# Forward transform of the Fourier tower: the third quarter of a pair's pixels is turned ahead of the first result of the pair in front

## The chip, the cores and the metric

The kernel runs on one core of a Trainium2 chip, as one launch. The metric is the device time of that launch in microseconds; lower is better. Three runs of the kernel before give a median of 4477.31 us (4468.72 to 4491.48).

## What is computed

A four-layer Fourier tower over 64 images of 64 x 64 pixels, followed by attention and expert layers on its result. All numbers are float32. The part that matters here is this, cut from the reference:

```python
for l in range(LAYERS):                       # LAYERS = 4
    sc = _spectral_conv(h, w1r[l] + 1j * w1i[l], w2r[l] + 1j * w2i[l])
    pw = jnp.einsum('bihw,oi->bohw', h, pw_w[l]) + pw_b[l][None, :, None, None]
    y = sc + pw
    y = (y - mean(y)) * rsqrt(var(y) + EPS) * gamma[l] + beta[l]
    h = jax.nn.gelu(y, approximate=False)
```

`_spectral_conv` takes the two-dimensional Fourier transform of h, keeps 32 x 16 of its modes, multiplies each mode by a 64 x 64 complex matrix and transforms back.

## The kernel before

The 64 images are 32 **pairs** (`NP`); one pair is 128 partitions x 4096 pixels (two images of 64 channels), 2 MB. Four pairs (`Q`) are a group. Each layer has three stages, with a barrier of all engines between them (`phase_end`): **forward** (Fourier transform of h), **mix** (the products per mode) and **inverse**. For layer 0 the forward transform is done in another way; so the loop over layers (`Fori(1, L)`) runs the forward stage three times. This case is about that stage alone: `sync_forward`, `tensor_forward`, `scalar_forward` and `vector_forward`, lines 717 to 822.

What is done for a pair p in the forward stage, in the order of the data:

1. SP loads the pair from `y_dram` into one of four buffers, `hf[p % 4]` (L721). The load of pair p waits until all four quarters of pair p - 4 have been turned out of that buffer.
2. ACT applies scale, shift and Gelu in place, in four quarters of 1024 columns (L790).
3. VectorE **turns** each quarter: `px_turn(p, v)`, v = 0 to 3, a transpose in blocks of 32 x 32 from `hf` to `hT[p % 2]` (L795).
4. PE does the transform along the width, `w_dft(p)`: 32 products in the program, 64 matmul records in the trace (L750). It starts when all four quarters are turned and both results of pair p - 1 have been taken from its banks 0 to 3.
5. VectorE takes the result in two halves: `w_turn(p, 0)` from banks 0 and 1, then `w_turn(p, 1)` from banks 2 and 3 (L800).
6. PE does the transform along the height, `h_dft(p)`, 128 matmul records, into banks 4 to 7 (L767). It starts when both halves of step 5 are taken.
7. VectorE takes that with two transposes, `h_turn(p)` (L809), and once in four pairs SP stores the group's spectrum to `spec_in` (L726).

Each engine runs its instructions in the order in which they are written. PE goes `w_dft(p)`, `h_dft(p - 1)`, `w_dft(p + 1)`, and so on. VectorE's order is the loop at the end of `vector_forward`. Its step p of 34 handles three pairs at once: the pixels of pair p, the width result of pair p - 1 and the height result of pair p - 2:

```python
for p in range(NP + 2):
    # px_turn(p, 0), px_turn(p, 1),
    # w_turn(p - 1, 0), px_turn(p, 2),
    # w_turn(p - 1, 1), h_turn(p - 2), px_turn(p, 3)
```

In the text below a **cycle** is the stretch from the end of one `px_turn(p, 3)` to the end of the next; there are 31 in each forward stage, 93 in all.

Of the kernel before, what the change touches and what calls it, by code (L numbers as in the profile page):

```python
# [102 lines left out]
def build(nc, d, B, out):  # L103

    NP, NG = B // 2, B // GI
# [3 lines left out]
    with ExitStack() as ctx:  # L109
# [682 lines left out]
        def vector_forward(dve, lf):  # L792
            def px_turn(p, v):
                dve.wait_ge(f_ready, lf * (NP * 4) + (p * 4 + v + 1))
                dve.transpose(hT[p % 2][:, :, 16 * v:16 * v + 16, :].rearrange("p s h c -> p h s c"),  # L795
                              hf[p % Q][:, v * 2 * BK:(v + 1) * 2 * BK].rearrange("p (h s x) -> p h s x", h=16, s=2)).then_inc(px_turned, 1)

            def w_turn(p, i):
                dve.wait_ge(wdft_done, lf * (NP * 4) + (p * 4 + 2 * i + 2))
                dve.transpose(t1[p % 2][:, 2 * i:2 * i + 2].rearrange("p g a c h -> p (g a) c h"),  # L800
                              banks[:, 2 * i:2 * i + 2, :].rearrange("p b (a h c) -> p (b a) c h", a=2, c=CQ)).then_inc(wdft_turned, 1)

            def h_turn(p):
                g, q = p // Q, p % Q
                dve.wait_ge(hdft_done, lf * NP + (p + 1))
                if q == 0:
                    dve.wait_ge(spec_stored[g % 2], lf * (NG // 2 * 16) + (g // 2 * 16 + 16))
                for b in range(2):
                    dve.transpose(xs[g % 2][:, :, b * Q + q, :, :],  # L809
                                  banks[:, 4:8, b * 128:(b + 1) * 128].rearrange("p q (c k) -> p k q c", c=CQ)).then_inc(hdft_turned, 1)  # L810

            for p in range(NP + 2):
                for v in range(2):
                    if p < NP:
                        px_turn(p, v)
                for i in range(2):
                    if 0 < p <= NP:
                        w_turn(p - 1, i)
                    if i == 1 and p > 1:
                        h_turn(p - 2)  # L820
                    if p < NP:
                        px_turn(p, 2 + i)

# [1121 lines left out]
        @block.vector  # L1947
        def _(dve):
            vector_spectrum0(dve)
            phase_end(dve, 1)  # L1950
            vector_mix(dve, 0, True)
            phase_end(dve, 2)
            vector_inverse(dve, 0, True)
            dve.sem_inc(px_turned, 4 * Q)
            dve.sem_inc(wdft_turned, 2)
            dve.sem_inc(hdft_turned, 2)
            phase_end(dve, 3)
            with dve.Fori(1, L) as l:
                vector_forward(dve, l - 1)
                phase_end(dve, l * 3 + 1)  # L1960
                vector_mix(dve, l, False)
                phase_end(dve, l * 3 + 2)
                vector_inverse(dve, l, False)
                phase_end(dve, l * 3 + 3)
            vector_head(dve)
            phase_end(dve, TOWER + 1)
            tail_vector(dve)
# [71 lines left out]
```

## Time and profile before

| | |
|---|---|
| median of three runs | 4477.31 us (4468.72 to 4491.48) |
| the profiled execution | 4476.43 us, its span 4474.6 us |
| mean granted TensorE clock | 0.884 of full speed |
| busy: PE, PE weight loads, DVE, ACT | 76%, 49%, 53%, 47% of the span |
| forward stages (by their VectorE instructions) | 663 to 983, 1574 to 1894, 2486 to 2810 us |
| DVE in them, three stages | L795 447.0 us, L800 235.6 us, L809 123.4 us |
| DMA | 1119.89 MB, 250 GB/s over the span |

The profile is one execution. Busy time is what an engine's instructions took; idle time is given with the instruction in front of which the engine sat, and with what ended the wait. A matmul record's end is modelled, so that records of neighbouring matmuls overlap. The granted clock is 1.00 at 2.4 GHz and 0.50 at 1.2 GHz; a value between them is a mean over the stretch. DVE is VectorE.

### The profile page before, as it was taken

Reading aid. Unit: us, or ns where it says so; the run is one execution under the profiler, and the core shown is the slowest. Engines: PE = TensorE matmul, PEld = TensorE weight load, DVE = VectorE, ACT = ScalarE, POOL = GpSimd, SP = SyncE. Lnnn points to the kernel's source line nnn. Section 1 sums busy time; section 2 is a strip of 40 time slices with the busy share of each in tenths; the row PEclk is TensorE's granted clock in tenths of the full one; section 3 lists DMA queues with packets and bytes.
Section 4 is the critical chain, followed back from the end, with each engine's and each line's share of the span. In section 5 each row is a group of like instructions: output and inputs, shape, how many; then the busy total and the mean of one; then the engine's idle time right before and its main releaser. Section 6 shows DMA issues by size and latency. Waiting matters only on the chain. (4 is left out here: it accounts for less than half of the span.)

```text
span 4474.6 us, 121788 instructions
## 1 busy us (share of the span) xinstructions
PE 3399.7 (76%) x54724; PEld 2181.0 (49%) x54724; DVE 2393.1 (53%) x3232; ACT 2098.7 (47%) x1724; POOL 28.9 (1%) x48
## 2 busy tenths in 40 slices
PE   4978866659788756597888466878887999569877
PEld 3856643438455534385555244665553222453532
DVE  3456657864465578734656688335652000454456
ACT  1223335522466655323666543226667999222321
POOL 0000000000000000000000000000000000100000
PEclk8999988889899878898989788989998999669788
DMA  6969876768899967597999675879996543003042
GB/s 243 355 180 246 227 236 247 292 235 332 303 394 382 353 236 292 220 360 281 382 385 358 257 272 218 345 267 393 383 365 244 193 172 114 11 2 76 1 97 66
DMA packets 217486, 1119.89 MB, mean 250 GB/s; under 512 B 24521, under 2 KB 96401, under 8 KB 139054
## 3 DMA queue, kind: packets, MB, share of 16 engines
q1 hardware_dynamic: 177070, 843.73, 51.3%
q10 hardware_dynamic: 38976, 268.98, 17.4%
q8 instruction: 332, 5.44, 0.5%
q0 software_dynamic: 1024, 1.05, 0.1%
q14 instruction: 84, 0.69, 0.0%
HBM read 708.56 MB, written 405.14 MB: 249 GB/s over the span
## 5 line engine op out<-in xcount | busy, mean ns | idle before, releaser
L552 PEld LDWEIGHTS bank<-fb,arena 64*64 64x64 f32 x16384 | 665.6, 199 | 456.8 <-issue 442.7
L552 PE MATMUL bank<-fb,arena 64*64 64x128 f32 x16384 | 671.8, 292 | 182.3 <-ACT arena L609 137.0
L609 ACT ACTIVATE arena<-bank,pwb 128x1024 f32<-128x1024 f32 x512 | 557.7, 1110 | 460.4 <-PE bank L543 352.0
L653 DVE BATCH_NORM_STATS2 stats<-arena 128x6 f32<-128x512 f32 x1024 | 625.8, 674 | 149.5 <-ACT arena L609 149.0
L397 PE MATMUL bank<-arena 128*32 128x128 f32 x8192 | 589.3, 475 | 105.7 <-DMA arena<-in_w_modes 105.7
L543 PE MATMUL bank<-arena,wst 64*64 64x512 f32 x4096 | 627.6, 626 | 26.5 <-issue 26.4
L790 ACT ACTIVATE arena<-arena,shift,scale 128x1024 f32<-128x1024 f32 x384 | 443.7, 1229 | 390.9 <-DMA arena<-y_dram 390.8
L397 PEld LDWEIGHTS bank<-arena 128*32 128x32 f32 x8192 | 510.6, 136 | 183.6 <-issue 107.1
L601 ACT ACTIVATE arena<-arena,shift,scale 128x2048 f32<-128x2048 f32 x192 | 401.5, 2092 | 394.7 <-issue 194.6
L645 DVE STREAM_TRANSPOSE arena<-bank 128x512 f32<-128x512 f32 x512 | 320.7, 683 | 491.6 <-PE bank L529 491.6
L750 PE MATMUL bank<-arena,fwq 32*32 32x512 f32 x6144 | 310.6, 830 | 356.8 <-DVE arena L795 356.8
L795 DVE STREAM_TRANSPOSE arena<-arena 128x1024 f32<-128x1024 f32 x384 | 447.0, 1202 | 16.7 <-ACT arena L790 16.7
L529 PE MATMUL bank<-arena,ga 64*64 64x512 f32 x2048 | 312.8, 635 | 121.9 <-DMA arena<-spec_out 104.8
L767 PE MATMUL bank<-arena,ghq 32*32 32x256 f32 x12288 | 351.7, 427 | 28.0 <-issue 23.5
L409 ACT ACTIVATE arena<-arena 64x4096 f32<-64x4096 f32 x32 | 127.4, 3980 | 491.8 <-DMA arena<-spec_in 491.8
L430 DVE STREAM_TRANSPOSE arena<-bank 128x512 f32<-128x512 f32 x256 | 160.8, 686 | 351.9 <-PE bank L397 351.9
L767 PEld LDWEIGHTS bank<-arena,ghq 32*32 32x32 f32 x12288 | 280.6, 111 | 120.0 <-issue 89.4
L750 PEld LDWEIGHTS bank<-arena,fwq 32*32 32x32 f32 x6144 | 97.6, 116 | 478.2 <-issue 469.3
L800 DVE STREAM_TRANSPOSE arena<-bank 128x1024 f32<-128x1024 f32 x192 | 235.6, 1228 | 115.5 <-PE bank L750 115.5
L866 PE MATMUL bank<-arena,fc 64*128 64x512 f32 x1024 | 265.5, 627 | 14.8 <-ACT arena L894 13.4
L901 ACT ACTIVATE arena<-bank,fc1b 128x1024 f32<-128x1024 f32 x256 | 267.8, 1122 | 14.3 <-PE bank L866 14.3
L529 PEld LDWEIGHTS bank<-arena,ga 64*64 64x64 f32 x2048 | 113.3, 140 | 246.0 <-issue 235.5
(195 smaller groups left out, 2354.2 us busy)
## 6 DMA issues: line engine op xcount, KB each, us to landing
arena<-y_dram SPq DMA_DIRECT2D x224, 2048.0 KB, 10.2
y_dram<-arena ACTq DMA_DIRECT2D x256, 1024.0 KB, 12.7
arena<-spec_in SPq DMA_DIRECT2D x32, 2048.0 KB, 7.9
arena<-in_w_modes SPq DMA_DIRECT2D x32, 2048.0 KB, 14.2
spec_out<-arena SPq DMA_DIRECT2D x64, 1024.0 KB, 15.8
arena<-spec_out SPq DMA_DIRECT2D x112, 512.0 KB, 20.2
spec_in<-arena SPq DMA_DIRECT2D x24, 2048.0 KB, 13.5
spec_in<-arena SPq DMA_DIRECT2D x4, 4096.0 KB, 20.8
```

Of the source, the lines that this page charges most:

```text
L397: mm = pe.matmul(bank[4 * v + k // 4][t * HB:(t + 1) * HB, k % 4 * 2 * B:(k % 4 + 1) * 2 * B], w_sb[u][:, mode, t // 2 * HB:(t // 2 + 1) * ...
L529: mm = pe.matmul(bank[2 * v + r][CHAN[par], :], ga[k_p, r * S:(r + 1) * S], grp[p // Q % 2][k_p, :, par * Q + q, :], start=True, stop=True ...
L543: mm = pe.matmul(bank[4 + T % 2 * 2 + i][CHAN[v], :], wst[CHAN[i], :], hin[p % 3][CHAN[i], px:px + BK], start=False, stop=True, tile_posit ...
L552: mm = pe.matmul(hpx(bank[4 + T % 2 * 2 + i][CHAN[v], :])[:, :, j * S:(j + 1) * S], a2[p % 2][CHAN[i], v, :, 4 * T + j], hpx(fb2[CHAN[i], :]),
L601: act.activation(x, x, ACT.Gelu, bias=shift[:], scale=scale[:]).then_inc(h_ready, 1)
L609: act.activation(hpx(yout[u])[:, :, T * BK:(T + 1) * BK], banks[:, 4 + T % 2 * 2:6 + T % 2 * 2, :], ACT.Identity, bias=pwb[:]).then_inc(y_ ...
L645: dve.transpose(a2[p % 2][:, :, v * HB + c0:v * HB + c0 + 16, :].rearrange("p v c r -> p c v r"), banks[:, 2 * v:2 * v + 2, :].rearrange(" ...
L653: dve.bn_stats(stats[:, p * 48 + 6 * t:p * 48 + 6 * t + 6], hpx(yout[p % 2])[:, i, T * BK:(T + 1) * BK]).then_inc(y_seen, 1)
L750: mm = pe.matmul(bank[g][QUAD[c], :], fwq[QUAD[g], s * 32:(s + 1) * 32], hT[q % 2][QUAD[g], s, :, c * CQ:(c + 1) * CQ], start=(s == 0), st ...
L767: mm = pe.matmul(bank[4 + c][QUAD[j], 0:256], ghq[QUAD[c], col:col + K1], t1[q % 2][QUAD[c], v:4:2, hh, :, ri * M2:(ri + 1) * M2], start=( ...
L790: act.activation(x, x, ACT.Gelu, bias=shift[:], scale=scale[:]).then_inc(f_ready, 1)
L795: dve.transpose(hT[p % 2][:, :, 16 * v:16 * v + 16, :].rearrange("p s h c -> p h s c"), hf[p % Q][:, v * 2 * BK:(v + 1) * 2 * BK].rearrang ...
```

## The change

VectorE's order within a step, and nothing else. `px_turn(p, 2)` and `w_turn(p - 1, 0)` change places; all other instructions keep theirs.

```diff
             for p in range(NP + 2):
-                for v in range(2):
+                for v in range(3):
                     if p < NP:
                         px_turn(p, v)
                 for i in range(2):
                     if 0 < p <= NP:
                         w_turn(p - 1, i)
-                    if i == 1 and p > 1:
-                        h_turn(p - 2)
-                    if p < NP:
-                        px_turn(p, 2 + i)
+                if p > 1:
+                    h_turn(p - 2)
+                if p < NP:
+                    px_turn(p, 3)
```

One step of VectorE's queue in the forward stage of the kernel before, from its `px_turn(p, 0)` on (L795 is a `px_turn`, L800 a `w_turn`, the two L809 an `h_turn`; the rows of L794 and L805 are the register arithmetic of their waits):

```order
L794 REGISTER_ALU
L795 STREAM_TRANSPOSE arena<-arena 128x16x2x32
L794 REGISTER_ALU
L795 STREAM_TRANSPOSE arena<-arena 128x16x2x32
L800 STREAM_TRANSPOSE arena<-bank 128x1024
L794 REGISTER_ALU
L795 STREAM_TRANSPOSE arena<-arena 128x16x2x32
L800 STREAM_TRANSPOSE arena<-bank 128x1024
L805 REGISTER_ALU
L809 STREAM_TRANSPOSE arena<-bank 128x8x64 x2
```

The same step of the changed kernel's VectorE queue, from `px_turn(p, 0)` on:

```order
L794 REGISTER_ALU
L795 STREAM_TRANSPOSE arena<-arena 128x16x2x32
L794 REGISTER_ALU
L795 STREAM_TRANSPOSE arena<-arena 128x16x2x32
L794 REGISTER_ALU
L795 STREAM_TRANSPOSE arena<-arena 128x16x2x32
L800 STREAM_TRANSPOSE arena<-bank 128x1024 x2
L805 REGISTER_ALU
L809 STREAM_TRANSPOSE arena<-bank 128x8x64 x2
```

The third L795 now stands in front of both L800, which follow each other; the two L809 and the step's last L795, which comes after them, stand where they stood. The queues of PE, ACT, SP and GpSimd are the same row by row, and so is the number of VectorE's instructions.

## Rows read from the trace of the kernel before

**Rows 1.** Groups by line, from the page: count, busy, mean ns, idle before, releaser.
```profile
L790 ACT ACTIVATE arena<-arena,shift,scale 128x1024 f32<-128x1024 f32 x384 | 443.7, 1229 | 390.9 <-DMA arena<-y_dram 390.8
L750 PE MATMUL bank<-arena,fwq 32*32 32x512 f32 x6144 | 310.6, 830 | 356.8 <-DVE arena L795 356.8
L795 DVE STREAM_TRANSPOSE arena<-arena 128x1024 f32<-128x1024 f32 x384 | 447.0, 1202 | 16.7 <-ACT arena L790 16.7
L767 PE MATMUL bank<-arena,ghq 32*32 32x256 f32 x12288 | 351.7, 427 | 28.0 <-issue 23.5
L800 DVE STREAM_TRANSPOSE arena<-bank 128x1024 f32<-128x1024 f32 x192 | 235.6, 1228 | 115.5 <-PE bank L750 115.5
L809 DVE STREAM_TRANSPOSE arena<-bank 128x512 f32<-128x512 f32 x192 | 123.4, 680 | 34.0 <-PE bank L767 33.3
```

**Rows 2.** Waits of DVE in the third forward stage: total us, times, longest.
```profile
DVE arena L800 <- PE bank L750: 41.2, 32, 2.5
DVE arena L809 <- PE bank L767: 9.8, 8, 2.9
DVE arena L795 <- ACT arena L790: 6.8, 1, 6.8
```

**Rows 3.** DVE in order of time, a cycle at full clock, then one partly at half.
```profile
754.06 3.46 DVE L795 STREAM_TRANSPOSE arena<-arena 128x1024 f32<-128x1024 f32 x3
757.77 1.25 DVE L800 STREAM_TRANSPOSE arena<-bank 128x1024 f32<-128x1024 f32 x1 [0.26 <-PE bank L750]
758.95 1.20 DVE L795 STREAM_TRANSPOSE arena<-arena 128x1024 f32<-128x1024 f32 x1
760.08 1.21 DVE L800 STREAM_TRANSPOSE arena<-bank 128x1024 f32<-128x1024 f32 x1
761.21 1.27 DVE L809 STREAM_TRANSPOSE arena<-bank 128x512 f32<-128x512 f32 x2
762.40 3.45 DVE L795 STREAM_TRANSPOSE arena<-arena 128x1024 f32<-128x1024 f32 x3
767.72 1.25 DVE L800 STREAM_TRANSPOSE arena<-bank 128x1024 f32<-128x1024 f32 x1 [1.86 <-PE bank L750]
...
771.15 1.27 DVE L809 STREAM_TRANSPOSE arena<-bank 128x512 f32<-128x512 f32 x2
772.34 3.45 DVE L795 STREAM_TRANSPOSE arena<-arena 128x1024 f32<-128x1024 f32 x3
```

**Rows 4.** Busy time in cycles: us, PE, PEld, DVE, ACT, POOL, PEclk, DMA share, GB/s.
```profile
755.26:763.60 8.34, 4.94 (x192) 3.69 (x192) 8.08 (x9) 4.16 (x5) 0.00 (x0) 1.00 0.69 252
763.60:773.55 9.95, 6.54 (x192) 3.84 (x192) 8.09 (x10) 5.92 (x6) 0.00 (x0) 0.83 0.57 211
891.89:900.99 9.10, 6.37 (x192) 4.47 (x192) 8.20 (x10) 4.01 (x4) 0.00 (x0) 0.78 0.94 386
2587.08:2597.45 10.37, 7.56 (x192) 4.65 (x192) 8.19 (x9) 4.80 (x5) 0.00 (x0) 0.66 0.55 202
```

**Rows 5.** DVE and PE in order of time, a cycle in which h_dft ends last.
```profile
692.16 1.25 DVE L800 STREAM_TRANSPOSE arena<-bank 128x1024 f32<-128x1024 f32 x1 [0.26 <-PE bank L750]
...
698.51 1.31 DVE L809 STREAM_TRANSPOSE arena<-bank 128x512 f32<-128x512 f32 x2 [2.84 <-PE bank L767]
699.75 3.45 DVE L795 STREAM_TRANSPOSE arena<-arena 128x1024 f32<-128x1024 f32 x3
...
697.24 1.24 PE L767 MATMUL bank<-arena,ghq 32*32 32x256 f32 x36 [3.10 <-issue]
```

**Rows 6.** ACT in order of time: the Gelu of pair 11.
```profile
754.29 4.64 ACT L790 ACTIVATE arena<-arena,shift,scale 128x1024 f32<-128x1024 f32 x4 [6.55 <-DMA arena<-y_dram]
```

**Rows 7.** DMA queues and issues from 755 to 970 us.
```profile
q1 hardware_dynamic: 9120, 54.53, 68.2%
q14 instruction: 4, 0.03, 0.0%
arena<-y_dram SPq DMA_DIRECT2D x20, 2048.0 KB, 8.4
```

**Rows 8.** PE in order of time: a `w_dft` at half clock behind a short gap.
```profile
901.24 4.08 PE L750 MATMUL bank<-arena,fwq 32*32 32x512 f32 x64 [2.72 <-DVE arena L795]
```

**Rows 9.** PE in order of time, the same two cycles as from 754 us above.
```profile
757.43 3.01 PE L767 MATMUL bank<-arena,ghq 32*32 32x256 f32 x127
763.85 3.83 PE L750 MATMUL bank<-arena,fwq 32*32 32x512 f32 x64 [3.40 <-DVE arena L795]
767.15 3.24 PE L767 MATMUL bank<-arena,ghq 32*32 32x256 f32 x128
```

**Rows 10.** DMA queue of instructions from 663 to 752 us.
```profile
q8 instruction: 11, 0.18, 0.7%
```

## The prediction

> **What bounds the kernel now.** I read the page's groups by line first, for the lines of the diff [rows 1]. VectorE's 192 `w_turn` (L800) are preceded by 115.5 us in which VectorE sat idle until the width transform L750 was done; the 384 `px_turn` (L795) by almost nothing. PE for its part waited 356.8 us at L750 until the pixels were turned. ACT waited 390.8 us for the loads from `y_dram`. So the first question is which of these engines sets the pace of a forward stage.
>
> The list of waits of one stage [rows 2] says how the idle time is spread: VectorE waits at L800 once per pair, 32 times, 41.2 us together (37.6 and 36.7 us in the other two stages), and at the height result L809 only 8 times, 9.8 us. Work in order of time then shows one cycle after the other. In the cycle from 754.06 to 762.40 VectorE is idle for 0.26 us alone [rows 3], and the granted clock is 1.00 [rows 4]: 8.34 us, of which VectorE's own work is all but 0.26. In the next, from 762.40 to 772.34, it waits 1.86 us at L800 [rows 3], with a granted clock of 0.83 [rows 4]: 9.94 us. In the cycle that ends in [rows 5] it waits 0.26 us at L800 and then 2.84 us at L809, since PE stood still in the middle of `h_dft` for 3.10 us with the releaser "issue". In both directions VectorE and PE wait for each other: PE starts `w_dft(p)` when pixel quarter 3 is turned, VectorE then turns pixel quarters of the next pair while it waits for the result. It is a loop of two engines, and a cycle is as long as the longer of two ways through it:
> - VectorE's own work, one after the other;
> - `w_dft`, `h_dft` on PE, then `h_turn` and the last `px_turn`, after which PE can start again.
>
> **ACT and the loads are not in the loop.** ACT's Gelu of pair 11 starts at 754.29 [rows 6]; VectorE turns that pair's first quarter at about 773.5 (the second of the three in the last row of [rows 3]), 19 us later. A load takes 8.4 us to land [rows 7] and the four Gelu quarters 4.64 us [rows 6]. With four buffers, a load has four cycles for that. If a cycle shrinks by 1 us, the 19 us shrink by about 4. ACT's long wait costs nothing before or after, and I cost the earlier loads at nothing: the cover is those 15 us. The DMA share in a cycle is 0.57 and 0.69 [rows 4].
>
> **The change, part by part.** Nothing is added or removed; one `px_turn` moves ahead of one `w_turn`.
>
> *The wait at L800.* After quarter 3 of pair p the work on VectorE was two quarters, now it is three. From the spacing of starts in [rows 3]: a `px_turn` takes 1.13 (758.95 to 760.08), a `w_turn` 1.18 and 1.13 (757.77 to 758.95, 760.08 to 761.21), an `h_turn` 1.19 (761.21 to 762.40). VectorE's own work in a cycle is 4 x 1.13 + 1.18 + 1.13 + 1.19 = 8.02 us. That is the floor of the new cycle. What is queued behind `w_turn(p, 0)`, now later by up to 1.13 us: PE needs both halves only for `h_dft(p)`, which stands behind `w_dft(p + 1)` in its queue, and that starts more than 4 us later. `w_turn(p, 1)` needs the second half of the result; at either clock the second half comes at most about 1.0 us after the first (a quarter of the 4.08 us of [rows 8]), and the first `w_turn` takes 1.18. So no new wait there.
>
> *The wait at L809.* `h_turn` keeps its place and comes earlier by the idle time saved, until `h_dft` is the last to end. In [rows 3, 9] the `h_dft` of the second cycle ends at 767.15 + 3.24 = 770.39.
>
> Three kinds of cycle follow. I went through all 93 in the order of time and sorted them.
> 1. **At full clock, 24 cycles of 8.34 us.** L800 waits 0.26. After: 8.02, bound by VectorE; the height result (757.43 + 3.01 = 760.44) [rows 9] is there before `h_turn` starts at 754.06 + 4.52 + 2.31 = 760.89, where 4.52 is four `px_turn` and 2.31 two `w_turn`. Gain 0.32 each: 24 x 0.32 = **7.7 us**.
> 2. **Partly at half clock, 44 cycles of 8.9 to 9.95 us, mean 9.46.** L800 waits 0.8 to 2.0. Worked for the second cycle of [rows 3]: the fourth `px_turn` since 762.40 would end its slot at 762.40 + 4.52 = 766.92, the result is there at 767.72, so L800 still waits 0.8; then 2.31 to 770.03, where L809 waits for 770.39 + 0.04; then 1.24 for `h_turn` when it has waited (698.51 to 699.75, [rows 5]), which gives 771.67 instead of 772.34. Gain 0.67. Where `w_dft` was less slow the saved idle is smaller and `h_dft` ends relatively later: the other members gain 0.1 to 0.7, and the 44 together 16.4 us, 0.37 each. The sum is **16.4 us**.
> 3. **`h_dft` ends last already, 25 cycles of 9.1 to 11.4 us.** These are pairs 2 to 7 of each stage with PE's "issue" stops [rows 5], cycles wholly at half clock and the ones like 891.89 to 900.99 [rows 4]. VectorE waits at L809 now, so an earlier `h_turn` is impossible. Gain **0**.
>
> With PE's timing kept as it is: 7.7 + 16.4 = 24.1 us, 0.54%.
>
> *PE's clock.* PE's idle stretch in front of `w_dft` is `h_turn`, the last `px_turn` and what lay idle: 3.40 us behind the full-clock cycle [rows 9]. In the changed kernel it is 0.32 us less there. The full-clock cycle behaves as it does although PE worked for 4.94 of 8.34 us; with 4.94 of 8.02 PE is busier, so I expect somewhat more of the time at 2.4 GHz. Each cycle of kind 2 that becomes kind 1 is worth 9.1 - 8.0 = 1.1 us. No row prices how many do; the ends are 0 and all 44 (48 us). Since [rows 8] show a `w_dft` wholly at half clock behind a gap of only 2.72 us, I stay near the low end, six of 44: **6.6 us**.
>
> The Trainium skill, TensorE: Matmul & The Clock Gate, section "HAM oscillation — how this bites in real kernels", says that bursts of matmuls separated by long enough idle gaps start at the low clock each time, and that shorter gaps cure it. By that rule all of kind 2 would go to 8.0; the row with 2.72 us speaks against it, so it is a rival below and not the sum.
>
> The "issue" stops come in the first pairs of a stage. From 755 to 970 us, under seven turns of PE's loop over groups, queue q8, which brings 11 packets of instructions from 663 to 752 us [rows 10], does not appear at all [rows 7] (4 packets of another queue are all), and I found no such stop there; a faster cycle thus doesn't meet them more often. The Trainium skill, Runtime: NRT & Kernel Launch, section "Instruction fetch mechanics", says that a taken branch to code outside the buffered window forces a fetch before the engine can go on. By it one cycle in four would carry a stop and gain nothing, and the sum would be 18 us; no row of that stretch shows it.
>
> *The ends of a stage.* The last two steps have no pixels to turn and do not change. Behind the last `h_turn` come the store and the barrier, as before; the mix stage starts earlier by the whole gain.
>
> **Sum:** 24.1 + 6.6 = 31 us off the profiled execution's 4476.4, that is 4445.7; the median of the runs shown is 0.9 us above that execution, so **4446 us** (-0.7%). Alone this case gives 4430 to 4460.
>
> **Rivals.**
> - *A: the second wait takes it all.* `h_dft` ends later than I read in kind 2, and L809 waits what L800 no longer does. For it: `h_turn` had under 0.8 us to spare in every cycle. Against: PE's records put its end before. The gain is then kind 1 alone or less, 0 to 10 us: 4467 to 4477. Chance 0.15.
> - *B: slower, through the clock.* In the third stage, from 2576.79 to 2607.71, three cycles in a row were 10.3 us each, with a granted clock of 0.66 [rows 4]: `w_dft` wholly at half speed each time. Such a run ended by itself after a few. If the shorter cycle makes it the standing state, a cycle is 10.3 instead of the mean 9.07 of kinds 1 and 2, +1.2 us. It decides from 20 further such cycles on (24.1 / 1.2); all 23 of one stage give +28 against -16 from the other two, +12 us (4489); all 68 give +84 us (4561). For it: the cycle would come out of PE alone and be tied more closely to the clock's own changes. Against: these cycles are bound by PE before and after the change alike, so they are no more stable than now, and PE is not idler. Chance 0.07.
> - *C: the clock stays up.* By the rule of the page on the clock gate: 44 x (9.46 - 8.02) = 63 us and 8 from kind 1: 71 us, 4406. For it: the gaps shrink. Against: [rows 8]. Chance 0.08.
> - *D: the change does less than it says* because ACT is late with quarter 2. ACT leads by 19 us except in the first cycle of a stage. Chance under 0.01.
>
> **How the numbers follow.** My case has 0.70, A 0.15, B 0.07, C 0.08. A change of 0.5% (22 us, to 4455) is about what a measurement of this kernel can tell from none. Of my case five sixths lie below 4455 (a clock term near zero, and the spread of runs of 20 us, take the rest), and C: 0.58 + 0.08 = 0.66. Slower by over 0.5%: most of B, 0.05. Within: 0.29. The range runs from 4422, a little over half the way to C, to 4472, most of A: what is left out is B, most of C and a little of A, 0.18.
>
> **What would show it.** Right: the idle time before L800 falls from 115.5 us [rows 1] to between 25 and 50, that before L809 rises from 34.0 [rows 1] to between 75 and 105 (80 saved, 24 of it gained, the rest waited there); full-clock cycles of 8.0 us alternate with ones of 9.0 to 9.2; the busy times of L795, L800 and L809 stay. The mean granted clock stays or rises a little over 0.884. Wrong: L809's idle grows by as much as L800's falls (A); cycles of 10.3 us in long runs (B); cycles of 8.0 us in long runs (C); a wait at L795 for ACT (D).

## The result, and the profile after

| | before | after |
|---|---|---|
| median of five runs | 4477.31 us (4468.72 to 4491.48) | 4442.24 us (4435.59 to 4455.82) |
| ratio | | 0.9919, 95% interval 0.9897 to 0.9940 |
| span of the profiled execution | 4474.6 us | 4433.7 us |
| three forward stages, first to last `px_turn(p, 3)` | 293.7 + 290.9 + 295.8 = 880.4 us | 277.7 + 278.8 + 277.8 = 834.3 us |
| mean granted clock | 0.884 | 0.888 |

The kernel is 0.8% faster, 35 us; 4446 us was forecast. (One execution of an experiment below, one quarter ahead, took 7491.72 us with most of its matmuls up to twice as long; it was disturbed and is left out.) The page's groups by line, after, for the lines of [rows 1]; the columns are count, busy, mean ns, idle before, releaser:

```profile
L790 ACT ACTIVATE arena<-arena,shift,scale 128x1024 f32<-128x1024 f32 x384 | 443.7, 1229 | 353.3 <-DMA arena<-y_dram 353.2
L750 PE MATMUL bank<-arena,fwq 32*32 32x512 f32 x6144 | 291.7, 778 | 334.9 <-DVE arena L795 334.9
L795 DVE STREAM_TRANSPOSE arena<-arena 128x1024 f32<-128x1024 f32 x384 | 440.0, 1203 | 15.3 <-ACT arena L790 15.3
L767 PE MATMUL bank<-arena,ghq 32*32 32x256 f32 x12288 | 347.7, 421 | 27.1 <-issue 22.6
L800 DVE STREAM_TRANSPOSE arena<-bank 128x1024 f32<-128x1024 f32 x192 | 226.8, 1219 | 27.7 <-PE bank L750 27.6
```

The height result's group of the same trace, from the groups by line:

```profile
L809 DVE STREAM_TRANSPOSE arena<-bank 128x512 f32<-128x512 f32 x192 | 124.6, 687 | 78.9 <-PE bank L767 78.9
```

VectorE's idle time at L800 fell from 115.5 us to 27.7, and that at L809 rose from 34.0 to 78.9. So of the 88 us that the first wait lost, 45 came back as the second. The difference, 43 us, is nearly all of what the forward stages gained (46 us). L795 shows 7 us less busy time with the same mean for one, and L800 9 us less with a mean only 9 ns lower: transposes that follow each other directly overlap in the records, now at one more place in a cycle for each of the two lines.

Two neighbouring cycles of VectorE after the change, in order of time, to be held against [rows 3]:

```profile
784.69 4.58 DVE L795 STREAM_TRANSPOSE arena<-arena 128x1024 f32<-128x1024 f32 x4
789.19 2.34 DVE L800 STREAM_TRANSPOSE arena<-bank 128x1024 f32<-128x1024 f32 x2
791.46 1.27 DVE L809 STREAM_TRANSPOSE arena<-bank 128x512 f32<-128x512 f32 x2
792.65 4.58 DVE L795 STREAM_TRANSPOSE arena<-arena 128x1024 f32<-128x1024 f32 x4
797.19 2.38 DVE L800 STREAM_TRANSPOSE arena<-bank 128x1024 f32<-128x1024 f32 x2
800.51 1.31 DVE L809 STREAM_TRANSPOSE arena<-bank 128x512 f32<-128x512 f32 x2 [0.94 <-PE bank L767]
```

And the busy time in two such cycles (columns as in [rows 4]):

```profile
776.79:785.89 9.10, 6.37 (x192) 4.08 (x192) 8.16 (x10) 4.63 (x4) 0.00 (x0) 0.81 1.06 429
785.89:793.85 7.96, 4.93 (x192) 3.59 (x192) 7.96 (x9) 4.87 (x5) 0.00 (x0) 1.00 0.76 284
```

The first L800 no longer waits. A cycle at full clock is 7.96 us and all VectorE; the next waits 0.94 us at L809 and is 9.1 us. The two kinds take turns through the rest of a stage, where the kernel before had 8.34 and 9.1 to 10.4 in an uneven order.

PE in the second of these cycles, to be held against the slow cycle of [rows 9]:

```profile
794.10 3.20 PE L750 MATMUL bank<-arena,fwq 32*32 32x512 f32 x64 [3.03 <-DVE arena L795]
796.28 4.19 PE L767 MATMUL bank<-arena,ghq 32*32 32x256 f32 x128
```

Here `w_dft` took 3.20 us and `h_dft` 4.19, where that slow cycle had 3.83 and 3.24. From the start of the one to the end of the other it is 6.37 us now and was 6.54 there; but more of the slow stretch lies in `h_dft`.

I sorted the cycles of both traces alike: the first seven of each stage, and of the other 72 those under 8.45 us (full clock) and the rest.

| | first 21, sum | full clock | the others | all 93 |
|---|---|---|---|---|
| before | 221.8 us | 24 of 8.35 | 48 of 9.55 | 880.4 us |
| after | 217.3 us | 36 of 7.96 | 36 of 9.18 | 834.3 us |

### The profile page after: what moved, and what is told of

Read it like the earlier page. It is cut to its first block and busy times, and to the rows that moved or that the text cites. A ratio compares the mean times of both kernels' runs of the same rounds, so it can differ in the third digit from the quotient of the medians.

```text
span 4433.7 us, 121788 instructions
## 1 busy us (share of the span) xinstructions
PE 3373.8 (76%) x54724; PEld 2206.0 (50%) x54724; DVE 2394.8 (54%) x3232; ACT 2099.7 (47%) x1724; POOL 29.0 (1%) x48
## 5 line engine op out<-in xcount | busy, mean ns | idle before, releaser
L397 PEld LDWEIGHTS bank<-arena 128*32 128x32 f32 x8192 | 545.3, 137 | 147.5 <-issue 107.1
L750 PE MATMUL bank<-arena,fwq 32*32 32x512 f32 x6144 | 291.7, 778 | 334.9 <-DVE arena L795 334.9
L795 DVE STREAM_TRANSPOSE arena<-arena 128x1024 f32<-128x1024 f32 x384 | 440.0, 1203 | 15.3 <-ACT arena L790 15.3
L800 DVE STREAM_TRANSPOSE arena<-bank 128x1024 f32<-128x1024 f32 x192 | 226.8, 1219 | 27.7 <-PE bank L750 27.6
```

The source lines that it names most:

```text
L397: mm = pe.matmul(bank[4 * v + k // 4][t * HB:(t + 1) * HB, k % 4 * 2 * B:(k % 4 + 1) * 2 * B], w_sb[u][:, mode, t // 2 * HB:(t // 2 + 1) * ...
L750: mm = pe.matmul(bank[g][QUAD[c], :], fwq[QUAD[g], s * 32:(s + 1) * 32], hT[q % 2][QUAD[g], s, :, c * CQ:(c + 1) * CQ], start=(s == 0), st ...
```

## The experiments

All are edits of the order in `vector_forward`, or of PE's work in `w_dft`. Each diff is against the changed kernel if nothing else is said. Times are medians; "before" is the kernel before, run beside them on the same chip.

### More of the order: h_turn last, and all four quarters ahead

```diff
-                if p > 1:
-                    h_turn(p - 2)
                 if p < NP:
                     px_turn(p, 3)
+                if p > 1:
+                    h_turn(p - 2)
```

> The step is three px_turn, both w_turn, then px_turn(p, 3), and h_turn(p - 2) last. My theory (a cycle is the longer of VectorE's own 8.0 us and the chain w_dft, h_dft, h_turn, last px_turn) says: h_turn leaves the chain, PE starts the next w_dft 1.2 us sooner and has a whole cycle for h_dft. All cycles after the first seven of a stage become 8.0 us, the idle time before L809 falls from 79 us to under 15, and the kernel is 35 to 60 us faster than the changed one: about 4385 to 4407 us. Rival (the height result is not what holds the 9.1 us cycles, their length is the clock's alone): cycles stay at 8.0 and 9.1 in turn, 4442 us within 10.

Measured: 4361.83 us against 4482.97 for the kernel before, ratio 0.9727 (0.9697 to 0.9758). The other version turns all four quarters, then takes both `w_turn`, then `h_turn`:

```diff
-                for v in range(3):
+                for v in range(4):
                     if p < NP:
                         px_turn(p, v)
...
-                if p < NP:
-                    px_turn(p, 3)
```

> The step is all four px_turn, both w_turn, h_turn(p - 2). w_dft(p) then waits for the w_turn of pair p - 1, not for pixels, and both of PE's results have several us to spare. My theory: cycles of 8.0 us, as with h_turn last, idle before L800 and L809 near 0 after the first seven pairs, 4385 to 4407 us; PE's clock no longer matters to the time. Rival (more quarters ahead only delay PE): w_dft starts 2.3 us later after the last quarter, cycles of 10 us or more, 4490 us or more.

Measured: 4355.04 us, ratio 0.9724 (0.9693 to 0.9755). Both beat both kernels of this case. One stretch of each, 120 us long (first `h_turn` last, then all ahead):

```profile
790.00:910.00 120.00, 81.25 (x2880) 56.50 (x2880) 120.00 (x121) 68.88 (x60) 0.00 (x0) 0.93 0.84 316
```
```profile
790.00:910.00 120.00, 81.80 (x2912) 55.82 (x2911) 120.00 (x121) 65.91 (x57) 0.00 (x0) 0.93 0.81 308
```

VectorE is busy for 120.00 of 120 us, although the granted clock is 0.93 and not 1.00. PE with `h_turn` last shows how; the same kernel, PE in order of time:

```profile
816.01 2.29 PE L750 MATMUL bank<-arena,fwq 32*32 32x512 f32 x61 [3.02 <-DVE arena L795]
...
823.97 3.45 PE L750 MATMUL bank<-arena,fwq 32*32 32x512 f32 x64 [3.02 <-DVE arena L795]
826.70 3.64 PE L767 MATMUL bank<-arena,ghq 32*32 32x256 f32 x128
831.93 1.66 PE L750 MATMUL bank<-arena,fwq 32*32 32x512 f32 x34 [1.59 <-DVE arena L795]
```

The `w_dft` at 823.97 and the `h_dft` behind it are slower, and the next `w_dft` still starts 7.96 us later: the slow pair only shortens PE's idle stretch, to 1.59 us. That is the theory of the two ways through the loop. `h_turn` and the last `px_turn` no longer stand between `h_dft` and the next `w_dft`, so the second way is short at either clock. (In the kernel's code `h_dft(p)` also waits until `h_turn(p - 1)` is done. In the kernel before and in the changed one that comes before the `px_turn` that starts `w_dft(p + 1)`, and so never holds PE; with `h_turn` last it comes 1.2 us behind that `px_turn`, while `w_dft` still runs.) The rivals of both runs fell: neither cycles of 9.1 us nor a late PE.

My number was too small, 35 to 60 us over the changed kernel where 80 and 87 came. The cycles after the first seven did as expected (69 of 72 at 7.96 us, 41 us less than after the change; 67 of 72 with all ahead). The rest came from the first seven of each stage, which I had left as they were: 177.9 us in sum with `h_turn` last, against 217.3 after the change. PE still stops there; the same kernel, PE in order of time:

```profile
700.19 1.24 PE L767 MATMUL bank<-arena,ghq 32*32 32x256 f32 x36 [3.22 <-issue]
701.12 3.48 PE L750 MATMUL bank<-arena,fwq 32*32 32x512 f32 x64
```

A stop of 3.22 us in the middle of `h_dft`, as in [rows 5], and the next `w_dft` comes right behind. With PE's 3 us of spare time in a cycle such a stop is mostly absorbed instead of added: the 21 first cycles are 11 us above 21 times 7.96, where they were 50 us above it after the change. Not all of it is absorbed, and so the idle time before L809 missed what I had written: 24.5 us with `h_turn` last (under 15 expected) and 31.3 with all ahead, of which 11 and 14 us lie in the first seven cycles of the stages, 2 and 8 in the few later ones that are longer than 7.96, and the rest behind the last cycle.

### Less of the order: one quarter ahead

```diff
-                for v in range(3):
-                    if p < NP:
-                        px_turn(p, v)
-                for i in range(2):
-                    if 0 < p <= NP:
-                        w_turn(p - 1, i)
+                if p < NP:
+                    px_turn(p, 0)
+                if 0 < p <= NP:
+                    w_turn(p - 1, 0)
+                if p < NP:
+                    px_turn(p, 1)
+                if p < NP:
+                    px_turn(p, 2)
+                if 0 < p <= NP:
+                    w_turn(p - 1, 1)
```

> The change in the other direction: one px_turn ahead of w_turn(p - 1, 0), two between the w_turn. Theory: VectorE sits idle for the whole width transform less 1.2 us; full-clock cycles become 9.5 us and the mean about 10.4 against 9.1 now: 24 x 3 x 1.3 = 90 us more than before, about 4570 us, idle before L800 near 220 us, idle before L809 near 10. Rival (PE's results set the pace, the place of w_turn does not matter): 4480 us.

The run took 4616.04 us, 46 us more than expected, without a usable profile. So it ran once more:

> One px_turn ahead of w_turn(p - 1, 0), once more, since the profile of the first try was of a disturbed execution; its other run took 4616 us. Theory: 4600 to 4620 us, idle before L800 over 200 us, the mean cycle after the first seven 10.5 us or more.

Measured: 4584.97 us (4581.01 to 4598.42), 103 us more than before, ratio 1.0234 (1.0200 to 1.0268). That is 15 us under the range that I gave, which came from the single run. Its group at L800:

```profile
L800 DVE STREAM_TRANSPOSE arena<-bank 128x1024 f32<-128x1024 f32 x192 | 235.6, 1228 | 250.3 <-PE bank L750 250.3
```

The idle time at L800 is 250.3 us, and the one at L809 16.8. The mean cycle after the first seven is 10.58 us, and not one was at 8.45 or less. With one, two, three and four quarters ahead the times are 4585, 4482, 4442 and 4355 us: the place of `w_turn` among the quarters is a cause by itself, and the rival (PE's results set the pace wherever `w_turn` stands) is out. The first three differ in the place of the first `w_turn` alone. The fourth also takes the last `px_turn` ahead of `h_turn`, which with three quarters ahead gives 80 of its 87 us already.

### PE's idle stretch filled

To part the order's share from the clock's, extra matmuls were put in PE's idle stretch. Their result is overwritten by `w_dft`. First 24 per pair, in the kernel before and in the changed one (the same edit in both):

```diff
-                pe.wait_ge(px_turned, n * 4 + (4 * Q + 4))
                 pe.wait_ge(wdft_turned, n * 2 + 2)
                 pe.sem_inc(waited[pe.engine], 1)
+                for r in range(24):
+                    c, j = r % 4, r // 4 % 4
+                    pe.matmul(bank[c][QUAD[j], 0:256], ghq[QUAD[c], 0:K1], ghq[QUAD[c], 0:256], start=True, stop=True,
+                              tile_position=(32 * c, 32 * j))
+                pe.wait_ge(px_turned, n * 4 + (4 * Q + 4))
+                pe.sem_inc(waited[pe.engine], 1)
```

> The kernel before, with 24 extra matmuls of 256 columns (48 records, about 1 us at full clock) in PE's idle stretch in front of every w_dft; their result is overwritten. If the clock falls because PE idles there, and the clock is what makes the 9.5 us cycles, all cycles after the first seven become 8.34 us with a granted clock of 1.00: 24 x 0.8 x 3 = 50 us less than before, about 4425 us. Rival (the low clock has nothing to do with the idle stretch, or the extra work delays w_dft): 4477 us or more.

> The changed kernel with the same 24 extra matmuls. If order and clock are separate causes, all cycles after the first seven become 8.0 us: 24 x 0.55 x 3 = 40 us less than the changed kernel, about 4403 us, and the difference to the kernel before with the same matmuls is the direct gain of the order at a steady clock, 72 x 0.32 = 23 us. Rival (the change gains through the clock alone): no difference between these two.

Measured: 4660.28 and 4657.93 us, 4% slower than before, both. The first lies within the "4477 us or more" of its rival, but neither expectation had the cause. DMA queues of the first of them, 755 to 960 us:

```profile
q8 instruction: 39, 0.64, 1.3%
arena<-y_dram SPq DMA_DIRECT2D x17, 2048.0 KB, 8.8
```

Queue q8 had brought nothing in that stretch in the kernel before [rows 7]. PE's loop over groups has 96 products per pair, two matmuls and two weight loads each, four pairs: 1536 such instructions; with the 24 it has 1920, and q8 brings about nine packets of 16 KB in each turn of 47 us. From this I take it that the code is fetched again in every turn. One cycle in four is then mostly 15 to 16 us long. I tried half of it:

> As the run with 24 extra matmuls in the kernel before, with 12 of them (three behind each other on each row of blocks, about 1.3 us at full clock), so that PE's loop body is 1728 instead of 1920 matmul and weight-load instructions. If the 24 cost their time through code that had to be loaded again in every turn of the loop (queue q8: 39 packets from 755 to 960 us where the kernel before had none), q8 has none again and the idle stretch is filled at last: cycles of 8.34 us at a clock near 1.00, about 4425 us. If filling the gap is itself the cost, 4500 us or more.

> The same 12 in the changed kernel. Order and clock as separate causes: cycles of 8.0 us, about 4405 us, and about 23 us less than the kernel before with the same 12. The change through the clock alone: equal to it.

Measured: 4654.09 and 4652.28 us, and q8 again with 39 and 42 packets. 1728 instructions are still too many, so these four runs give no price for the clock. That each pair came out equal, as the rival "no difference between these two" had it, is not that rival's doing: both kernels of a pair are held up by the code. Then 3 per pair, all on one block of 32 x 32, where the loop has 1584:

> The kernel before with 3 extra matmuls behind each other on one block in PE's idle stretch, about 1.3 us at full clock and only 48 more instructions in the loop body. First: queue q8 brings no instructions from 755 to 960 us, other than with 12 or 24 extra matmuls. Then, if the idle stretch makes the clock fall, cycles after the first seven are 8.3 us at a clock near 1.00, the kernel about 4425 us. Rival (one busy block of sixteen does not hold the clock): cycles of 8.3 and 9.5 us as before, about 4480 us.

> The changed kernel with the same 3. Order and clock as separate causes: cycles of 8.0 us, about 4405 us, about 23 us less than the kernel before with the same 3. The change through the clock alone: equal to it. If the clock is not held: about 4440 us, as the changed kernel.

Measured: 4489.05 us in the kernel before, ratio to it 1.0011 (0.9993 to 1.0030), and 4448.66 in the changed one, ratio 0.9917 (0.9887 to 0.9946). Queue q8 is quiet, with 1 and 2 packets, though the 3 are busy for 1.45 us in each idle stretch and the 12 were for 1.50: what cost 4% was the number of instructions and not the filling. PE is now busy for most of the time, and yet the clock is what it was; from 790 to 920 us, the changed kernel without and with the 3:

```profile
790.00:920.00 130.00, 86.53 (x2935) 58.15 (x2908) 122.54 (x122) 71.79 (x62) 0.00 (x0) 0.89 0.82 304
```
```profile
790.00:920.00 130.00, 106.12 (x3006) 65.72 (x3007) 123.51 (x124) 72.04 (x63) 0.00 (x0) 0.91 0.83 309
```

So the rival that was on record for this pair held: work on one block of sixteen does not keep the clock up. Both kernels keep their pattern of cycles (25 and 35 of the 72 at full clock, where it was 24 and 36 without the extra work), and the change is worth 40 us here, about as much as without it. Last, the same with the whole array:

```diff
+                for r in range(3):
+                    pe.matmul(bank[0][:, 0:256], ident[:], ghq[:], start=True, stop=True)
```

> The changed kernel with 3 extra matmuls in PE's idle stretch that use all 128 x 128 of the array (identity times a constant of 256 columns), as long as the 3 on one block before. Theory now: what holds the clock is how much of the array works, not how long; then every w_dft starts at full clock, the cycles after the first seven are all 8.0 us at a granted clock near 1.00, and the kernel is 72 x 0.6 = 35 to 45 us faster than the changed one, about 4405 us. Rival (work in that stretch does not hold the clock, whatever its width; its fall has another cause): 8.0 and 9.1 us in turn, 4440 to 4450 us.

The waits are those of the diff above. Measured: 4407.63 us, ratio to the kernel before 0.9816 (0.9777 to 0.9855), 35 us under the changed kernel's 4442. The same stretch, and PE in order of time:

```profile
790.00:920.00 130.00, 106.10 (x3304) 76.16 (x3274) 130.00 (x131) 75.22 (x65) 0.00 (x0) 1.00 0.86 324
```
```profile
857.90 1.53 PE L747 MATMUL bank<-ghq,ident 128*128 128x256 f32 x6 [0.70 <-DVE arena L803]
860.22 2.29 PE L753 MATMUL bank<-arena,fwq 32*32 32x512 f32 x61 [0.79 <-DVE arena L798]
```

With the same 106 us of busy time as the narrow work the granted clock is 1.00, `w_dft` takes 2.29 us every time, and 69 of 72 cycles are 7.96 us. This shows that the 9.1 us cycles of the changed kernel come from the low clock: hold it up and they are gone. The narrow work, with the same waits and as many instructions, left them in place. Here VectorE is busy for 130.00 of 130 us.

### The changed kernel once more

> The changed kernel once more, for a second profile. If the stretches between the forward stages, which came out 8.3, 6.2 and -8.7 us longer than in the kernel before, belong to the change, they do so again; if they are the spread from one execution to the next, they come out otherwise, and the three forward stages are again 277 to 279 us each (first to last px_turn(p, 3)).

Measured: 4428.99 us (4411.34 to 4464.17), ratio 0.9899 (0.9836 to 0.9963). The stretches from the last `px_turn` of a stage to the first of the next, and from the last one to the end, are:

```
                 1st to 2nd   2nd to 3rd   to the end
before             614.0        617.6       1686.3 us
after              622.3        623.8       1677.7
after, again       617.5        613.0       1682.4
```

They differ by up to 11 us from one execution of the same kernel to the next, in both directions: spread, not a cost of the change. The forward stages are 282.5, 279.0 and 279.1 us, 840.6 in sum: the first, with its stops in the first seven cycles, is outside the 277 to 279 I had written, and the third by 0.1. (The first seven cycles of the three stages sum to 221.9 us, as before the change.) The other 72 cycles repeat: 35 at 7.96 and 37 at 9.19 us.

## Why the prediction was right

- **What bounds a forward stage**, a loop of VectorE and PE with two ways through it: right. The runs with `h_turn` last and with all quarters ahead remove the second way and leave VectorE busy all the time.
- **Full-clock cycles, 8.02 us forecast:** measured 7.96. The gain is 0.38 instead of 0.32 each, 9.1 us for the 24 instead of 7.7.
- **The others, 0.37 us each at PE's own timing:** measured 9.55 to 9.18, 0.37. I had it from 44 cycles (16.4 us); over the 48 outside the first seven, at their new mean, it is 18 us. That the two numbers agree is in part luck, since PE's timing did not stay: the worked cycle left 0.8 us of waiting at L800, and the 36 slow cycles after the change wait 0.16 us there on average and 0.83 at L809, with a faster `w_dft` and a slower `h_dft` (the two rows of PE above).
- **Cycles in which `h_dft` ends last already, no gain:** the first seven of each stage gave 4.5 us in one profile of the changed kernel and none in the other. Right. In the first of these profiles L800 lost 19 us of idle time in these cycles, and 15 came back at L809.
- **PE's clock, 6 cycles turned and 6.6 us:** under-sized. Twelve more cycles were at full clock than before, and each is worth 9.18 - 7.96 = 1.22 us: 14.6 us. The direction was right; the number six was a choice near the low end, since [rows 8] showed a slow `w_dft` behind a short gap. The run with the whole array filled shows the rest of this term: the 71 us that rival C had as a pure effect of the change need extra work in the gap as well, which took another 35 us off, 70 us in all.
- **The sum.** 9.1 + 18 + 14.6 + 4.5 = 46 us is what the forward stages gained in the profiled execution, against 31 forecast; the second profile of the changed kernel has 40. The medians show 35. The difference in that pair of profiles lies in the stretches between the stages, where executions of one kernel differ by as much (5.2 us there), and in the spread of runs. So the median agreed better than the working deserves, which is luck: the clock's term was less than half of what it came to.
- **The waits:** L800 at 27.7 us (25 to 50 forecast), L809 at 78.9 (75 to 105). Cycles of 8.0 and 9.1 in turn, as written.
- **Rivals.** A: the second wait took 45 of 88 us, not all. B: no row of cycles of 10.3 us after the first seven. C: not by this change alone. D: the wait for ACT at L795 is 15.3 us, the first quarter of each stage, as before; from its start on a pair's first quarter to VectorE's, ACT still led by 14 us or more from pair 4 of a stage on. In pairs 1 to 3 (counted from 0) that lead is only some 1, 4 and 10 us (1, 6 and 11 before), where I gave 19 us for all but the first cycle; still no wait came of it.
- **The instruction fetch:** that a shorter cycle does not meet more stops was right: q8 brought 11, 11 and 11 packets in the first 90 us of the three stages, and 11, 11 and 12 before. The rule of the Trainium skill (Runtime: NRT & Kernel Launch, "Instruction fetch mechanics"), by which each turn of the loop would stall, does not show for a body of 1536 or 1584 matmul and weight-load instructions; it does for 1728 and 1920.

What stays open: how the clock is set exactly. Narrow work did not hold it and wide work did; in between, on four blocks, there are only the runs that the code fetches disturbed. Why fast and slow cycles take turns so regularly after the change was not tested. The wide work was not put into the kernel before, so the share of the order at a steady clock is known only from the full-clock cycles of both kernels (8.35 and 7.96 us). And `h_turn` was not moved last without the change.

## What to carry to other kernels

When two engines wait for each other in a loop, follow both ways round it before you price a move: with the engines' own timing unchanged the first wait's idle time is an upper bound, and the second wait can take back a good part of what it loses (here 45 of 88 us). Ask then which instruction stands between the late result and the start of the next piece on the other engine. Moving work into the visible wait gave 35 us; moving that one as well (`h_turn` behind the last `px_turn`) gave 80 more, since it hid the slow clock (41 us in the forward stages) and most of PE's stops in their first cycles (39 us).

## What the runs showed of the hardware

- **Code of a loop on PE.** With 1536 and 1584 matmul and weight-load instructions in the loop's body, queue q8 brought 0 to 2 packets in some 200 us; with 1728 and 1920 it brought 39 to 42, one cycle in four went to 15 to 16 us, and the kernel to 4% over before. The 192 or 384 more instructions of these bodies went with 174 and 177 us in the kernel before, where 48 more went with 7 us or nothing (ratio 1.0011, 0.9993 to 1.0030). The Trainium skill, Runtime: NRT & Kernel Launch, "Instruction fetch mechanics", gives PE room for 2048 instructions and calls it a FIFO with sequential prefetch and no instruction cache that would profit from locality; the traces show the body reused from turn to turn up to somewhere between 1584 and 1728 of its matmuls and weight loads (its waits and branches are not counted in these numbers).
- **The width of the extra work decided the clock.** About 1.5 us of extra matmuls in every gap left the granted clock at 0.91 when they used one block of 32 x 32, and brought it to 1.00 when they used the whole array, with the same busy time of 106 us in 130. The Trainium skill, TensorE: Matmul & The Clock Gate, "HAM oscillation — how this bites in real kernels", tells of idle gaps alone; by the trace a gap filled with narrow work counts as one too.
- **Useless work can pay.** The three wide matmuls per pair took 35 us off the changed kernel. Removing the dependence on the clock by order paid more (80 us with `h_turn` last, 87 with all quarters ahead). Most of that difference is not the clock's: after the first seven cycles of a stage the wide work saved 32 us and `h_turn` last 41; in the first seven the wide work saved 2 us and `h_turn` last 39.
